# Second experts: the first layer's rows formed turned, its weights sent for each tile, the bias added with the relu

## The reference, cut to what matters

```python
combine = jax.nn.one_hot(flat_e, E, dtype=xt.dtype) * (g_prob * e_prob)[:, None]
h = jax.nn.relu(jnp.einsum('td,edf->etf', xt, w1) + b1[:, None, :])
y = jnp.einsum('etf,efd->etd', h, w2) + b2[:, None, :]
out = jnp.einsum('te,etd->td', combine, y)
...
x = _layernorm(x + moe_out, ln2_g, ln2_b)
```

## Time and profile before

| | |
|---|---|
| median of 3 runs | 2336.19 us (2335.84 to 2337.26) |
| the profiled execution's own time | 2329.9 us |
| its span in the profile | 2328.0 us |
| TensorE busy | 2007.7 us, 86% of the span |
| VectorE busy | 1515.2 us, 65% |
| ScalarE busy | 1217.3 us, 52% |
| GpSimd busy | 1175.0 us, 50% |
| mean granted TensorE clock | 0.947 of full speed |
| DMA | 213.13 MB, 92 GB/s on the mean |

### The profile page before, as it was taken

How to read it: one execution, slowest core, us unless ns; L and a number is a source line. 1 busy time by engine, 2 the same in 40 slices (tenths; PEclk the granted TensorE clock), 3 DMA queues, 4 the chain that set the end, 5 groups by cost and what they waited for, 6 DMA issues and landing times. The chain is left out here.

```text
span 2328.0 us, 35623 instructions
## 1 busy us (share of the span) xinstructions
PE 2007.7 (86%) x12048; PEld 1162.1 (50%) x12048; DVE 1515.2 (65%) x3263; ACT 1217.3 (52%) x2836; POOL 1175.0 (50%) x987
## 2 busy tenths in 40 slices
PE   7999899989999999985677994999999999773997
PEld 3555555555555555552344783444444444331765
DVE  4348767786868687775953554566677766454776
ACT  5576676666666666652112341566666666440221
POOL 2008566574747476673674543333344332235776
PEclk9999999999999999997889997899999999995999
DMA  8315443425200000004134553223333321212222
GB/s 273 107 55 193 158 147 114 151 91 180 71 25 1 20 1 19 1 14 148 48 108 134 172 181 91 58 66 98 84 92 102 116 55 37 71 37 98 82 88 74
DMA packets 183931, 213.13 MB, mean 92 GB/s; under 512 B 23401, under 2 KB 161513, under 8 KB 183498
## 3 DMA queue, kind: packets, MB, share of 16 engines
q1 hardware_dynamic: 132634, 130.15, 18.0%
q0 software_dynamic: 16752, 45.84, 6.5%
q10 hardware_dynamic: 34368, 34.87, 4.4%
HBM read 83.75 MB, written 114.46 MB: 85 GB/s over the span
## 5 line engine op out<-in xcount | busy, mean ns | idle before, releaser
L2045 DVE TENSOR_REDUCE m_mx<-ps 128x2 f32<-128x1024 f32 x256 | 313.3, 1224 | 191.0 <-PE ps L1980 189.5
L735 DVE CUSTOM_DVE_ANT_0 pb<-ps,bias,snl 128x128 f32<-128x128 f32 (+3 forms) x512 | 260.2, 546 | 226.4 <-PE ps L580 225.5
L853 POOL TENSOR_TENSOR prod<-qs,kvs 128x1024 f32<-128x1024 f32 x120 | 283.7, 2392 | 161.9 <-issue 142.3
L2115 ACT ACTIVATE m_pt<-ps 128x1024 f32<-128x1024 f32 x256 | 261.5, 1024 | 169.6 <-PE ps L1988 163.1
L853 POOL TENSOR_TENSOR prod<-sc,kvs 128x1024 f32<-128x1024 f32 x120 | 280.3, 2368 | 99.4 <-ACT sc L971 85.8
L931 ACT ACTIVATE pb<-pb,mst 128x129 f32<-128x129 f32 (+3 forms) x512 | 283.4, 560 | 19.1 <-DVE mst L735 17.0
L580 PE MATMUL ps<-kz,qT 64*128 64x128 f32 (+3 forms) x1024 | 186.2, 442 | 0.0
L865 DVE TENSOR_REDUCE sc<-prod 128x64 f32<-128x1024 f32 x128 | 152.2, 1209 | 43.6 <-POOL prod L853 43.3
L591 PE MATMUL ps<-ident,pb 128*128 128x128 f32 x1280 | 179.1, 279 | 0.5 <-DVE mst L735 0.4
L946 ACT ACTIVATE ptb<-ps 128x384 f32<-128x384 f32 (+1 forms) x256 | 135.4, 545 | 65.8 <-PE ps L591 65.2
L591 PEld LDWEIGHTS ps<-ident,pb 128*128 128x128 f32 x1280 | 140.2, 141 | 55.7 <-issue 43.3
(11 more groups left out here) (340 smaller groups left out, 4304.9 us busy)
## 6 DMA issues: line engine op xcount, KB each, us to landing
xh_scratch<-zt SPq DMA_DIRECT2D x43, 768.0 KB, 7.7
xe_scratch<-zt ACTq DMA_DIRECT2D x32, 1024.0 KB
ye_scratch<-e_ys SPq DMA_DIRECT2D x36, 256.0 KB
hw_w<-in_w SPq DMA_DIRECT2D x16, 512.0 KB
xin<-in_x SPq DMA_DIRECT2D x8, 512.0 KB
y_scratch<-e_y SPq DMA_DIRECT2D x8, 512.0 KB
m_x<-y_scratch SPq DMA_DIRECT2D x8, 512.0 KB
x1c_scratch<-e_x SPq DMA_DIRECT2D x8, 512.0 KB
```

The lines of the kernel that those rows point to most:

```text
L735: dv.tensor_tensor_reduce(pb.ap[:, j, SEG[t]:SEG[t] + n], rS.of(("S", b, p, t, j)).ap[:, 0:n], k.bias[:, h, CAUSAL[t]:CAUSAL[t + 1]], -1.0 ...
L853: e.tensor_tensor(out, one, two, ALU.mult).then_inc(*k.c.did(*product_done(step, b, t, u)))
L2045: dv.tensor_reduce(x.ap[:, t, 64 * half:64 * half + 64].rearrange("p (i r) -> p i r", i=2)[:, :, 2], score_ring(k, b, g, t, half).of((b, g ...
L2115: ac.activation(p.ap[:, 2 * half:2 * half + 2, :], k.qE.of((b, g, kt, half)).ap, ACT.Exp).then_inc(*did("m_exp", b, g, kt, half))
```

## The change

- The first layer of the second experts swaps its operands. For each quarter f of the 512 hidden columns and each half c of the 256 inputs, a 128x128 block of w1 is the stationary operand and the turned rows (128 columns) are the moving one. The result is the hidden rows already turned, so the turns of `h_hb` go, with the `hT4` ring. The hidden rows of a tile now take places in two PSUM banks at a time (`k.hH`, banks 2-3 and 4-5).
- w1 isn't kept in SBUF. SyncE reads the tile's expert number and loads its w1 (512 KB) into a ring of 3 buffers, tiles 0, 1 and 2 in step 0 and then tile j+2 in step j, once the first layer of tile j-1 is done.
- b1 is laid out by the host as 128 x 32; bias and relu are one ScalarE instruction for each quarter, with the bias read by a register address. VectorE's addition goes.
- Everything behind the first layer moves one step earlier: second layer of tile j-2, relu of j-1, statistics of j-2, result of j-3, store of j-4, residual of j, power of j-2. There are 43 steps in place of 44.
- In part three the eight w1 loads go, w2's stay (two for each period), and b1's load is 16 KB.

```diff
-    load = [x for e in range(E8) for x in (("g_w1", e), ("g_w2", e))] + [("g_b1",)]
+    load = [("g_w2", e) for e in range(E8)] + [("g_b1",)]
     for i, x in enumerate(load):
-        if i // 4 == b - 1:
-            out[4 + 8 * (i % 4)].append(x)
+        if i // 2 == b - 1:
+            out[4 + 16 * (i % 2)].append(x)
...
-            sp.dma_start(k.b1[:, :], row(ins["b1"].rearrange("x f -> (x f)"))).then_inc(*did("d_hw", E8, 0))
+            sp.dma_start(k.b1[:, :], ins["b1"]).then_inc(*did("d_hw", E8, 0))
...
-    return [("h_more",)] + [("h_expert", j) for j in range(NS_H + 5)] + [("h_end",)]
+    return [("h_more",)] + [("h_expert", j) for j in range(NS_H + 4)] + [("h_end",)]
...
-    k.hhb = Ring([sb(f"h_hb{i}", [P, F]) for i in range(2)])
+    k.w1 = Ring([sb(f"hw_w1{i}", [P, 2, F]) for i in range(3)])
...
-    k.hX, k.hH, k.hT4, k.hD = [Ring(bank[i:i + 2]) for i in (0, 2, 4, 6)]
+    k.hX, k.hH, k.hD = Ring(bank[0:2]), Ring([Cell(k.ps[:, i:i + 2, :], *bank[i].over) for i in (2, 4)]), Ring(bank[6:8])
...
+        elif step == "h_expert":
+            j = key[0]
+            for n in range(3) if j == 0 else [j + 2]:
+                if n < NS_H:
+                    t = k.w1.take(n, at("h_h", n, 3))
+                    w.wait_ge(at("h_tei", 0), t.room)
+                    r = sp.value_load(k.htei[0:1, n:n + 1], min_val=0, max_val=E8 - 1)
+                    sp.dma_start(t.ap[:, :, :], ins["w1"][bass.ds(r, 1)].rearrange("o (c p) f -> p (o c) f", p=P)).then_inc(*did(f"d_w1{n % 3}", n))
...
-                t, m = k.hsT.of(n), k.hH.take(("e", n), at("h_hb", n))
-                w.wait_ge(at("h_sT", n), at("d_hw", E8, 0), m.room)
-                for c in range(2):
-                    i = pe.matmul(m.ap, t.ap[:, c, :], k.w1[:, bass.ds(k.hreg[n], 1), c * F:(c + 1) * F].rearrange("p o f -> p (o f)"),
-                                  start=(c == 0), stop=(c == 1))
-                i.then_inc(*did("h_h", n))
-            if 0 <= j - 3 < NS_H:
-                n = j - 3
+                t, m = k.hsT.of(n), k.hH.take(("e", n), at("h_relu", n, 3))
+                w.wait_ge(at("h_sT", n), at(f"d_w1{n % 3}", n), m.room)
+                for f in range(4):
+                    for c in range(2):
+                        i = pe.matmul(m.ap[:, f // 2, f % 2 * P:(f % 2 + 1) * P],
+                                      k.w1.of(n).ap[:, c, f * P:(f + 1) * P],
+                                      t.ap[:, c, :], start=(c == 0), stop=(c == 1))
+                    if f % 2:
+                        i.then_inc(*did("h_h", n, f))
+            if 0 <= j - 2 < NS_H:
+                n = j - 2
...
-            if 0 <= j - 2 < NS_H:
-                n = j - 2
-                q, m = k.hhb.of(n), k.hT4.take(("e", n), at("h_relu", n))
-                w.wait_ge(at("h_hb", n), m.room)
-                for f in range(4):
-                    i = pe.transpose(m.ap[:, f * P:(f + 1) * P], q.ap[:, f * P:(f + 1) * P], ident[:, :])
-                i.then_inc(*did("h_hT_t", n))
...
-                dv.tensor_tensor(q.ap[:, :], k.hH.of(("e", n)).ap, k.b1[:, bass.ds(k.hreg_v[n] * F, F)], ALU.add).then_inc(*did("h_hb", n))
...
+            if 0 <= j - 1 < NS_H:
+                n = j - 1
+                w.wait_ge(at("h_tei", 0))
+                r = ac.value_load(k.htei[0:1, n:n + 1], min_val=0, max_val=E8 - 1)
+                t, m = k.hhT.take(n, at("h_o", n)), k.hH.of(("e", n))
+                for f in range(4):
+                    w.wait_ge(at("h_h", n, f // 2 * 2 + 1), at("d_hw", E8, 0), t.room)
+                    ac.activation(t.ap[:, f, :], m.ap[:, f // 2, f % 2 * P:(f % 2 + 1) * P], ACT.Relu, bias=k.b1[:, bass.ds(r * 4 + f, 1)]).then_inc(*did("h_relu", n, f))
...
-            if 0 <= j - 5 < NS_H:
-                n = j - 5
+            if 0 <= j - 4 < NS_H:
+                n = j - 4
...
-            if 0 <= j - 1 < NS_H:
-                n = j - 1
+            if j < NS_H:
+                n = j
```

More of the change, by code:

```diff
@@ L1762, in setup_three @@
     k.order3 = order_three()
-    k.w1, k.w2 = sb("hw_w1", [P, E8, 2 * F]), sb("hw_w2", [P, E8, 4 * D])
-    k.b1 = sb("hw_b1", [P, E8 * F])
+    k.w2 = sb("hw_w2", [P, E8, 4 * D])
+    k.b1 = sb("hw_b1", [P, E8 * 4])
     k.mbq = sb("m_bq", [P, G4])
@@ L1865, in sync_three @@
             sp.dma_start(k.x2d[b * NT + t], k.zb[t].of((b, t)).ap[:, :]).then_inc(*did(f"d_x2_{t}", b, t))
-        elif step == "g_w1":
-            x = key[0]
-            sp.dma_start(k.w1[:, x, :].rearrange("p (c f) -> p c f", c=2), ins["w1"][x].rearrange("(c p) f -> p c f", p=P)).then_inc(*did("d_hw", x, 0))
         elif step == "g_w2":
@@ L2329, in tensor_four @@
                 k.hreg[n] = pe.value_load(k.htei[0:1, n:n + 1], min_val=0, max_val=E8 - 1)
-                t, m = k.hsT.of(n), k.hH.take(("e", n), at("h_hb", n))
-                w.wait_ge(at("h_sT", n), at("d_hw", E8, 0), m.room)
-                for c in range(2):
-                    i = pe.matmul(m.ap, t.ap[:, c, :], k.w1[:, bass.ds(k.hreg[n], 1), c * F:(c + 1) * F].rearrange("p o f -> p (o f)"),
-                                  start=(c == 0), stop=(c == 1))
-                i.then_inc(*did("h_h", n))
-            if 0 <= j - 3 < NS_H:
-                n = j - 3
+                t, m = k.hsT.of(n), k.hH.take(("e", n), at("h_relu", n, 3))
[9 more added lines that the diff above has]
+                n = j - 2
                 t, m = k.hhT.of(n), k.hD.take(("e", n), at("h_yb", n))
-                w.wait_ge(at("h_relu", n), m.room)
+                w.wait_ge(at("h_relu", n, 3), at("d_hw", E8 - 1, 1), m.room)
                 for f in range(4):
@@ L2369, in vector_four @@
                 k.hreg_v[n] = dv.value_load(k.htei[0:1, n:n + 1], min_val=0, max_val=E8 - 1)
-                q = k.hhb.take(n, at("h_hT_t", n))
-                w.wait_ge(at("h_h", n), at("d_hw", E8, 0), q.room)
-                dv.tensor_tensor(q.ap[:, :], k.hH.of(("e", n)).ap, k.b1[:, bass.ds(k.hreg_v[n] * F, F)], ALU.add).then_inc(*did("h_hb", n))
-            if 0 <= j - 4 < NS_H:
-                n = j - 4
+            if 0 <= j - 3 < NS_H:
+                n = j - 3
                 z, l = k.hz.of(n), k.lnh[n // 2 % 3]
@@ L2571, in scalar_four @@
             if j < NS_H:
-                t = k.hsT.take(j, at("h_h", j))
+                t = k.hsT.take(j, at("h_h", j, 3))
                 w.wait_ge(at("h_sT_t", j), t.room)
                 ac.activation(t.ap[:, :, :], k.hX.of(("e", j)).ap[:, 0:D].rearrange("p (c k) -> p c k", c=2), ACT.Copy).then_inc(*did("h_sT", j))
-            if 0 <= j - 2 < NS_H:
-                n = j - 2
-                t = k.hhT.take(n, at("h_o", n))
-                w.wait_ge(at("h_hT_t", n), t.room)
-                ac.activation(t.ap[:, :, :], k.hT4.of(("e", n)).ap.rearrange("p (f k) -> p f k", f=4), ACT.Relu).then_inc(*did("h_relu", n))
+            if 0 <= j - 1 < NS_H:
[6 more added lines that the diff above has]
+                    ac.activation(t.ap[:, f, :], m.ap[:, f // 2, f % 2 * P:(f % 2 + 1) * P], ACT.Relu, bias=k.b1[:, bass.ds(r * 4 + f, 1)]).then_inc(*did("h_relu", n, f))
 def gpsimd_four(k, po, w, order):
@@ L2820, in layout @@
         "w_expert": a["L0_ffn_w_expert"], "b_expert": a["L0_ffn_b_expert"].reshape(8),
-        "w1": a["L0_ffn_w1"], "b1": a["L0_ffn_b1"], "w2": a["L0_ffn_w2"], "b2": a["L0_ffn_b2"],
+        "w1": a["L0_ffn_w1"], "b1": col(a["L0_ffn_b1"].reshape(-1), E8 * 4), "w2": a["L0_ffn_w2"], "b2": a["L0_ffn_b2"],
     }
```

## The result

The changed kernel takes 2348.88 us (median of 5 runs, 2344.22 to 2353.25) against 2337.26 (2335.84 to 2341.66) of the kernel before, timed side by side: a ratio of 1.0039, 95% interval 1.0024 to 1.0054. It is slower by 0.39%, clear of noise, and outside the range. A second timing on another chip, where the kernel before takes 2306.93 us, gave 1.0037 (1.0024 to 1.0050). Absolute times differ from chip to chip and, by up to 20 us, from execution to execution of one kernel, so from here on a kernel's time is told as its ratio to the kernel before on the same chip; 0.1% is 2.3 us. One execution of the kernel before, on the chip of e5 to e8, took 2889.86 us at a granted clock of 0.64; no ratio holds it.

What follows compares the result with a forecast made beforehand. GpSimd was taken to bound the second experts at 4.37 us a tile. Head -1.3 and run and tail -2.3 summed to -3.6 us, giving 2332.6 us (-0.15%, chance 0.50), with a range of 2329.5 to 2347.

Steps and rivals of the forecast that it cites:

- Which engine bounds: Second experts: GpSimd sets the pace at 4.37 us a tile, before and after the change, above TensorE's 4.10.
- TensorE's 3.71 us a tile: Second experts: TensorE's time a tile falls from 4.10 us to 3.71, at most 3.93, with a first layer of 1.76.
- The third rival: TensorE becomes the bound: 16 weight loads in series make a tile 5.5 us, +43, 2376 us; or clock down; chance 0.04.
- SyncE's loads: Second experts: each tile's 512 KB w1 load needs some 7 us against 11.3 available, so it is hidden.
- a rival at 0.20: Stores land late because w1 loads fall on them, past 1.13 us of slack; 2350 or 2341 us; chance 0.20.
- full price: Late stores: a store behind the whole load, 1.6 us, 0.5 over slack in some 34 steps: +17, 2350 us.
- the half price: Late stores: a longer period shifts the load away from the store, so half the cost, 2341 us, is as likely.
- Head: Start of the second experts, up to the first power: -2.3 gained, +1.0 for tile 0's late weights, -1.3 us in all.
- Run: Second experts, first power to the last gather's end: 144.2 us, against 141.5 before.
- Tail: Second experts, last gather's end to the last store's issue: 21.9 us for 7 stores, against 26.9 for 8 before.
- The attention stage: Loses eight 512 KB loads and the 2 MB spread of the bias; priced at nothing, between -1 and +1 us.
- GpSimd isn't the bound: Second experts: each tile takes 3.7 us, 39 x 0.4, -16, 2320 us; chance 0.03.

Runs made afterwards that it cites:

- e5: Changed kernel with the attention stage's eight w1 loads and 2 MB spread of b1 put back, read by nobody; 1.0086 of the kernel before.
- e8: e3 with the power taken off GpSimd, replaced by VectorE's reciprocal and ScalarE's square root; 0.9934 of the kernel before.
- e11: Kernel before with the power taken off GpSimd, replaced by VectorE's reciprocal and ScalarE's square root; 0.9941 of the kernel before.
- e12: e8 with ScalarE's w1 copy for tile j+1 moved right behind the turned rows of tile j; 0.9880 of the kernel before.
- e9: Changed kernel once more, unedited, timed beside e10 on the same chip; 1.0037 of the kernel before.
- e10: Changed kernel with only the 2 MB spread of the bias put back into the attention stage, read by nobody; 1.0063 of the kernel before.
- e6: Changed kernel with each tile's w1 load sent as four transfers of 128 KB, same bytes; 1.0046 of the kernel before.
- e3: Changed kernel with w1 kept in SBUF and ScalarE copying each tile's part into the ring, in place of SyncE's load; 1.0000 of the kernel before.
- e7: Changed kernel with SyncE's load for tile j+2 also waiting for VectorE's scaled sum of tile j-2; 1.0014 of the kernel before.

## Why the prediction was wrong, step by step

- **Which engine bounds**, right: GpSimd at 4.37 us a tile, undisturbed periods still so in the changed kernel, and e11 shows the bound lifted to TensorE's 4.10.
- **TensorE's 3.71 us a tile**, right: 3.73 (e12), where the 16 records of a first layer take 1.79 us up to the second layer's start, so the 16 weight loads add nothing in series. The third rival is out.
- **SyncE's loads, "hidden"**: this is the step that failed. The working asked whether a load arrives in time for its reader (7 us against 11.3: it does; no row shows TensorE held by w1 in the run), and let that stand as its cost. What a load costs others was put into a rival at 0.20. That rival is what happened, by its own place and about its price: a load on the store, the wait for the last store, over 1.13 us of slack. It gave +17 at full price. Idle time ahead of stores was 19.7 us in the first profile, 14.6 in e9's, 13.3 in e10's and 12.4 in e5's. That its 2350 us lie next to the measured 2348.88 is partly luck: the head's loss and the attention stage's gain, neither of them in it, came on top. It was foreseen at "some 34 steps" of 0.5 us; it came as 15 steps of 0.4 to 2.8. A load is 1.3 us of all engines as a whole transfer (1.6 was the estimate), and its packets spread over 2 us and more where other transfers run. That each long period moves the next load to another place in the next one, so that stores are hit in turns, fits the records; no run tests it.
- **Its chance** was the mistake, more than its price. The row that spoke for it, a first gather 1.1 us late under the b2 load, was called "just at the edge", and the half price, 2341, was thought as likely as the full one. The Trainium skill's "DMA: Bandwidth & Descriptors" (Queues, rings and completion order) says that an engine drains a whole packet of one ring before it switches. The trace of the changed kernel is in line with that (a store's first packet at 3.36 us in place of 1.62); e6 is so only in part, since smaller transfers let the first packet in earlier and left the landings as late, and no record names a packet's engine, so the switching itself isn't shown.
- **Head**, -1.3 forecast, +0.7 measured. The turned form gives 2.4 (e3; forecast 2.3). The three loads take 3.1 of it (18.84 against 15.76), where 1.0 was taken and 4.2 the bound. They did not hold the first layer by w1 itself, as forecast: the packets of tile 0's w1 were through at 2140.2. They held it by the rows. TensorE turned tile 0 at 2139.74, 6.4 us after the gather's issue (4.99 before), and the turn of tile 1, which stands ahead of tile 0's first layer in its stream, waited for rows until 2141.34, 6.7 us after their gather, with the DMA share at 1.0 from 2138.

```profile
2139.74 0.66 PE L2329 MATMUL ps<-ident,h_xs 128*128 128x128 f32 x2 [17.78 <-DMA h_xs<-xh_scratch,h_gix]
...
2141.34 0.69 PE L2329 MATMUL ps<-ident,h_xs 128*128 128x128 f32 x2 [0.94 <-DMA h_xs<-xh_scratch,h_gix]
...
2142.10 3.75 PE L2339 MATMUL ps<-h_sT,hw_w 128*128 128x128 f32 x16
```

- **Run**, 144.2 forecast, 163.0 measured: 19.7 of idle ahead of stores accounts for all of it; without the stalls it is 143.3.
- **Tail**, 21.9 forecast, 22.9 measured (22.7 to 24.8 in the other three profiles of that form, 26.3 to 27.2 in the three with the old one): the step saved there is real.
- **The attention stage**, priced at nothing within 1 us: the gain was of another size. Put back, the loads cost some 0.5% by the medians (e5), between 0.2 and 0.8%. Without this gain the change would have lost about twice as much. That no wait of TensorE was found on those loads said too little; what they slow down there, no run shows.
- **A slip in the sums**: the case "GpSimd isn't the bound" subtracts its 16 us from 2336 and not from the forecast; from 2332.6 it is 2317. It decides nothing.

## What to carry to other kernels

A transfer that is early enough for its reader is not free: ask which other transfer moves its rows in the same microseconds, and whether an engine that sets the pace waits for that one. If such a meeting can't be avoided, move the transfer in time (e7) or fetch from SBUF (e3); cutting it into pieces did nothing here (e6). And before making an engine faster, look whether it sets the pace: the turned form was worth nothing until GpSimd had lost its power and ScalarE's copy stood at another place, and 11 us after.

## What the runs showed of the hardware that I had not expected

- A 2 KB packet of a load takes 0.084 us and a 1 KB packet 0.046, so a load in rows of 1 KB holds the engines 10% longer (e6, the changed kernel).
- The granted clock dropped inside the run in e3. TensorE stood idle for 0.86 and 1.97 us between 2215 and 2218.4, and then the clock was at its lower level (1.2 GHz) for a part of the next stretch, so that a first layer took 2.82 us in place of 1.95 (columns as in the earlier trace rows, the clock is the third last):

```profile
2214.00:2218.00 4.00, 1.60 (x10) 1.15 (x9) 1.30 (x5) 0.96 (x4) 3.18 (x5) 1.00 0.31 99
2218.00:2222.00 4.00, 3.57 (x14) 3.08 (x15) 2.89 (x8) 3.05 (x9) 2.83 (x4) 0.71 0.26 70
```

  The kernel before kept 1.00 through its whole run, the changed one 0.98. It is part of the 4.8 us that powers waited in e3; how much, no run here separates.
- A GpSimd store is issued in 1.00 us where no power precedes it and in 1.06 where one does, and the gap ahead of it is 0.30 in place of 0.18: without the power the period falls by 0.55 us, to 3.82 (the undisturbed ones of e12), not by the 0.93 that the expectation of e8 took.
